# Crossing the half sums of G: one batch of the pair on ScalarE, the other on VectorE

## The chip, the cores and the metric

The kernel runs on one core of one Trainium2 chip. The metric is the device time of one execution in microseconds. Three runs of the kernel before took 2286.35, 2272.86 and 2268.79 us; their median is 2272.86.

## The reference

The input x holds 32 batches of 64 channels by 1024 positions, with one style vector of 128 numbers per batch. Four layers follow one another, each x = x + ffn(cond(x)). All four conditioning stages have the same form, four modulated 1-D convolutions of 64 channels with 3 taps:

```python
def _layer(x, style, w, b, mw, mb, typ):
    s = style @ mw.T + mb
    weight = SCALE * w * s[:, None, :, None]
    demod = lax.rsqrt(jnp.sum(weight * weight, axis=(2, 3)) + EPS)
    weight = weight * demod[:, :, None, None]
    ...
for i, typ in enumerate(('same', 'upsample', 'same', 'downsample')):
    out = _layer(out, style, weights[i], biases[i], mod_w[i], mod_b[i], typ)
```

The feed-forward stages differ: layer 0 multiplies by a 1024x1024 matrix after rounding both sides to fp8, layer 1 adds a two-of-16 expert low-rank term to a dense product, layer 2 a sparsemax mixture of 8 low-rank experts, layer 3 is a low-rank gated unit (1024 to 256 to 2 x 2752 to 256 to 1024).

## The kernel before, in words

The batches are handled in 16 pairs; a tile of 128 rows holds 64 channels of both batches, or two position parities of one batch. Each layer runs `conv_phase`, then (layers 0, 1 and 3) a phase of its own for the feed-forward part; in layers 1 and 2 the dense product is done inside `conv_phase`.

In `conv_phase` the last three convolutions of a batch are folded into one filter G, which depends on the batch. Per pair TensorE does: `conv0` (first convolution, two halves), `weights_a` and `weights_g` (products that build G; `weights_g` writes one batch's G to PSUM bank 5 and the other's to bank 6, as two half sums that lie in the other 64 rows, shifted by 64 columns), `main_half` (the filter G over the signal, 12 matmuls of 512 columns per batch), `transpose_h`, and from layer 1 on `ffn`. Every fp32 operand is split in a high and a low part (`..._hi` by ScalarE, `..._lo` by VectorE or GpSimd), and three products are summed.

The half sums of G are brought together in three steps. `cross_g` on ScalarE copies 64 rows of both banks to the other 64 rows of the SBUF tile `g_f`, twice (lines 1056 and 1057, 64x896 each). `sum_g` on VectorE (line 1239) waits for both copies and adds the banks to `g_f`, 128x1024. `split_g` then makes G's high part on ScalarE (line 1061) and its low part on VectorE (line 1243, `gl_ready`), for which `main_half` of that pair waits.

Every engine's order is written out by hand, in `iteration` of each engine's block, and waits are semaphores. In iteration p TensorE runs `main_half(p, 0)`, `weights_g(p + 1)`, `main_half(p, 1)`, half of `conv0(p + 1)`, `transpose_h(p)`, the other half, `weights_a(p + 2)` and `ffn(p)`. ScalarE: `read_a(p + 1)`, `split_x(p + 1)`, `split_z(p + 2)`, in layer 0 `quantise`, `read_h(p, 0)`, `cross_g(p + 1)`, `read_h(p, 1)`, in layer 0 `split_g(p + 1)`, `read_u(p + 1, 0)`, `split_h(p)`, `read_u(p + 1, 1)`, in the other layers `split_g(p + 1)`, `tail`. VectorE keeps the same order with its own halves of these steps, `sum_g(p + 1)` standing behind `quantise` in layer 0 and behind `split_z` elsewhere; in layer 0 `split_g(p + 1)` follows at once, and `split_h(p)` is the `hmax` reduction (line 1254) for which the next `main_half` waits (`hl_ready`).

The first pair of a layer is different. `cross_g(0)` and `sum_g(0)` stand ahead of it, and TensorE's `edges_p` (line 807) waits for `g_summed`, because it reuses banks 5 and 6. `first_pair` on VectorE then works off the edge windows (`edges_p`, `edges_v`, `edges_y`), chunks of the layer's dense weights (line 1267) or, in layer 0, the maxima of the fp8 weights, and has `sum_g(1)` between them. GpSimd makes the low part of the first chunks (line 1551) and patches edges into `hs`.

Of the kernel before, what the change touches and what calls it, by code (L numbers as in the profile page):

```python
# [29 lines left out]
ACT = mybir.ActivationFunctionType  # L30
# [5 lines left out]
P = 128  # L36
B = 32
C = 64
# [3 lines left out]
HALF = 512  # L42
# [17 lines left out]
TAPS7 = 7 * C  # L60
# [3 lines left out]
def wait_pos(eng, sem, value):  # L64

    if not isinstance(value, int) or value > 0:
        eng.wait_ge(sem, value)
# [100 lines left out]
def program(nc, d, xs):  # L168

    with ExitStack() as root:  # L170
# [12 lines left out]
        for layer in range(DEPTH):  # L183
            with ExitStack() as keep:
# [30 lines left out]
                writes_x = layer in (1, 2)  # L215
                pack = packs[layer] if layer < 3 else None
                conv_phase(nc, layer, d, xs[nbuf], xs[nbuf + 1] if writes_x else None, pack, K, kept, sem, steps, ps)
                nbuf += writes_x
                if layer == 0:
# [282 lines left out]
def conv_phase(nc, layer, d, x_src, x_dst, pack, K, kept, sem, steps, ps):  # L502
# [7 lines left out]
    g0 = NP * layer  # L510
# [4 lines left out]
    with ExitStack() as ctx:  # L515
        def sb(name, shape, dt=F32):
            return ctx.enter_context(nc.sbuf_tensor(lay + name, shape, dt))
# [14 lines left out]
        g_f = sb("g_f", [P, 2, HALF])  # L532
# [108 lines left out]
        a_done, ah_ready, al_ready = sem("a_done"), sem("ah_ready"), sem("al_ready")  # L641
        c0_done, uh_ready, ul_ready = sem("c0_done"), sem("uh_ready"), sem("ul_ready")
        g_done, gh_ready, gl_ready = sem("g_done"), sem("gh_ready"), sem("gl_ready")
        g_crossed, g_summed = sem("g_crossed"), sem("g_summed")
        m_done, hs_ready, hs_patched = sem("m_done"), sem("hs_ready"), sem("hs_patched")
        t_done, hh_ready, hl_ready = sem("t_done"), sem("hh_ready"), sem("hl_ready")
        x_loaded = sem("l0_x_loaded" if layer == 0 else "x_loaded")
# [376 lines left out]
        def _(act):  # L1024
# [27 lines left out]
            def cross_g(p):  # L1052

                act.wait_ge(g_done, 2 * (g0 + p) + 2)
                wait_pos(act, gl_ready, g0 + p)
                nc.scalar.activation(g_f[0:C, :, C:HALF], ps[C:P, 5:7, 0:TAPS7], ACT.Copy).then_inc(g_crossed, 1)
                nc.scalar.activation(g_f[C:P, :, 0:TAPS7], ps[0:C, 5:7, C:HALF], ACT.Copy).then_inc(g_crossed, 1)  # L1057

            def split_g(p):
                act.wait_ge(g_summed, g0 + p + 1)  # L1060
# [58 lines left out]
            split_x(1)  # L1119
            some_chunks(1)  # L1120
            cross_g(0)
            some_chunks(1)
            split_g(0)
# [7 lines left out]
            def first_pair():  # L1131
                some_chunks(1)
                read_a(1)
                some_chunks(1)
                split_z(2)
                read_u(1, 0)
                read_u(1, 1)
                some_chunks(2)
                act.wait_ge(ey_ready, n)
                if layer == 0:  # L1140
                    act.wait_ge(sem("p_packed_away"), 48)
                read_h(0, 0)
                read_h(0, 1)
                cross_g(1)
                if layer > 0:
                    some_chunks(1)
                else:
                    split_g(1)
                split_h(0)
                if layer > 0:  # L1150
                    some_chunks(1)
                    split_g(1)
                some_chunks(len(chunks))
                if layer > 0:
                    tail(0)

            def iteration(p, first, ahead):
                if first:
                    first_pair()
                    return  # L1160
                if ahead:
                    read_a(p + 1)
                    split_x(p + 1)
                if ahead > 1:
                    split_z(p + 2)
                if layer == 0:
                    quantise(p - 1)
                read_h(p, 0)
                if ahead:
                    cross_g(p + 1)  # L1170
                if layer == 3:
                    tail_p(p - 1)
                read_h(p, 1)
                if ahead:
                    if layer == 0:
                        split_g(p + 1)
                    read_u(p + 1, 0)
                split_h(p)
                if ahead:
                    read_u(p + 1, 1)  # L1180
                    if layer > 0:
                        split_g(p + 1)
                elif with_ffn:
                    next_weights()
                if layer > 0:
                    tail(p)
# [13 lines left out]
        def _(dve):  # L1200
# [3 lines left out]
            v = nc.vector  # L1204
# [30 lines left out]
                                       ALU.subtract).then_inc(ul_ready, 1)  # L1235

            def sum_g(p):
                dve.wait_ge(g_crossed, 2 * (g0 + p) + 2)
                v.tensor_tensor(g_f[:, :, :], ps[:, 5:7, :], g_f[:, :, :], ALU.add).then_inc(g_summed, 1)  # L1239

# [95 lines left out]
            dve.wait_ge(zeros_ready, 2 * layer + 2)  # L1336
            edges_u()
            sum_g(0)
            split_x(1)
            split_g(0)  # L1340
# [106 lines left out]
            def first_pair():  # L1447
                edges_p()
                read_a(1)
                split_z(2)  # L1450
                if layer > 0:
                    some_chunks(1)
                edges_v()
                read_u(1, 0)
                read_u(1, 1)
                edges_y()
                some_chunks(2)
                sum_g(1)
                if layer == 0:
                    split_g(1)  # L1460
                    for k in range(KB):
                        wmax(k)
                    dve.wait_ge(side[0], KB)
                    v.tensor_reduce(qm[:, 0:1], wamax[:, :], AX_X, ALU.max).then_inc(side[4], 1)
                some_chunks(1)
                split_h(0)
                if layer == 0:
                    dve.wait_ge(side[4], 2)
                    step(v.tensor_scalar(kept["w_inv"][:, :], qm[:, 1:2], 1e-12, 1.0 / FP8_MAX, ALU.max, ALU.mult))
                    v.reciprocal(wr[:, :], kept["w_inv"][:, :]).then_inc(side[3], 1)  # L1470
                else:
                    split_g(1)
                    some_chunks(len(chunks))
                    tail(0)

            def iteration(p, first, ahead):
                if first:
                    first_pair()
                    return
                if ahead:  # L1480
                    read_a(p + 1)
                    split_x(p + 1)
                if ahead > 1:
                    split_z(p + 2)
                if layer == 0:
                    quantise(p - 1)
                if ahead:
                    sum_g(p + 1)
                    if layer == 0:
                        split_g(p + 1)  # L1490
                if layer == 3:
                    tail_p(p - 1)
                if ahead:
                    read_u(p + 1, 0)
                split_h(p)
                if ahead:
                    read_u(p + 1, 1)
                    if layer > 0:
                        split_g(p + 1)
                elif with_ffn:  # L1500
                    next_weights()
                if layer > 0:
                    tail(p)
# [767 lines left out]
```

## Time and profile before

| | us |
|---|---|
| median of three runs | 2272.86 |
| profiled execution | 2273.95 |
| its span | 2272.1 |
| TensorE busy | 2043.1 (90%) |
| VectorE busy | 1192.0 (52%) |
| ScalarE busy | 880.9 (39%) |
| GpSimd busy | 428.7 (19%) |

The profile is that of one execution. The convolution phases lie roughly at 57 to 300 us (layer 0), 445 to 830 (layer 1), 1090 to 1550 (layer 2) and 1560 to 1825 (layer 3). Busy shares are averages over phases with different limits, so each place that the change touches has to be read by itself. A row's idle time is that of the engine just before the instruction, and the arrow names what ended it.

### The profile page before, as it was taken

How to read it: one execution, taken by the hardware profiler on the slowest of the kernel's cores; microseconds unless marked ns; L12 is line 12 of the kernel's file. 1: busy time of each engine (PE TensorE's matmuls, PEld its weight loads, DVE VectorE, ACT ScalarE, POOL GpSimd, SP SyncE). 2: the span in 40 equal slices, each digit the busy share in tenths (PEclk: the TensorE clock that was granted, in tenths of full speed). 3: DMA queues.
4: the chain of work that ended last, by engine and by line, in shares of the span. 5: the costliest groups of instructions: out<-in, count | busy, mean ns of one | idle time of the engine just before them, and what ended most of it. 6: DMA issues, size and time to landing. Idle time of an engine off the chain costs nothing. (4 is left out here: it accounts for less than half of the span.)

```text
span 2272.1 us, 29864 instructions
## 1 busy us (share of the span) xinstructions
PE 2043.1 (90%) x9740; PEld 1668.4 (73%) x9748; DVE 1192.0 (52%) x1999; ACT 880.9 (39%) x1352; POOL 428.7 (19%) x481
## 2 busy tenths in 40 slices
PE   2579956689999998999799999997999999979998
PEld 2458842368888886888688888876888878858886
DVE  5668769875545544232754444446555534454443
ACT  2358741144434432000433333332666644423442
POOL 4112214411001110110211111111000023352334
PEclk9889988889999998999899999997999999989999
DMA  5243314522112113222421111212111011132113
GB/s 141 84 133 100 108 51 148 189 103 69 55 55 77 61 47 120 93 92 93 144 75 55 55 55 65 73 48 80 28 37 34 22 44 48 48 111 97 43 48 152
DMA packets 98093, 180.72 MB, mean 80 GB/s; under 512 B 21120, under 2 KB 50816, under 8 KB 97280
## 3 DMA queue, kind: packets, MB, share of 16 engines
q1 hardware_dynamic: 96768, 178.16, 24.7%
q10 hardware_dynamic: 1280, 1.97, 0.4%
q8 instruction: 27, 0.44, 0.1%
q14 instruction: 18, 0.15, 0.0%
HBM read 126.02 MB, written 45.68 MB: 76 GB/s over the span
## 5 line engine op out<-in xcount | busy, mean ns | idle before, releaser
L907 PE MATMUL ps<-l_u_hi,l_g_hi 128*128 128x512 f32 x512 | 209.1, 408 | 28.8 <-DVE hmax L1254 27.6
L1065 ACT ACTIVATE l_hs<-ps,l_EY,dem3e 128x512 f32<-128x512 f32 x128 | 99.0, 777 | 296.3 <-PE ps L907 285.9
L907 PE MATMUL ps<-l_u_lo,l_g_hi 128*128 128x512 f32 x512 | 205.5, 401 | 0.0
L907 PE MATMUL ps<-l_u_hi,l_g_lo 128*128 128x512 f32 x512 | 205.0, 400 | 0.0
L119 POOL TENSOR_TENSOR l_hs<-l_EY,ones 128x4 f32<-128x4 f32 x128 | 30.7, 241 | 796.9 <-ACT l_hs L1065 796.9
L960 PE MATMUL ps<-l_w_hi,l_h_hi 128*128 128x512 f32 x512 | 167.4, 408 | 0.0
L2202 POOL TENSOR_TENSOR f_a_lo<-f_prod,f_a_hi 128x512 fp32r<-128x512 f32 (+1 forms) x88 | 113.5, 1290 | 269.4 <-ACT f_a_hi L2105 269.4
L960 PE MATMUL ps<-l_w_lo,l_h_hi 128*128 128x512 f32 x512 | 163.8, 401 | 0.0
L960 PE MATMUL ps<-l_w_hi,l_h_lo 128*128 128x512 f32 x512 | 163.0, 400 | 0.0
L2158 DVE SCALAR_TENSOR_TENSOR f_prod<-ps,b,f_gate 128x512 f32<-128x512 f32 (+1 forms) x88 | 66.0, 750 | 170.2 <-ACT f_gate L2098 170.2
L851 PE MATMUL ps<-l_x_hi,c_hi 128*128 128x512 f32 x256 | 110.5, 432 | 40.0 <-POOL l_u_lo L1533 39.7
L1233 DVE SCALAR_TENSOR_TENSOR l_u_lo<-ps,s_u,l_u_hi 128x512 fp32r<-128x512 f32 x128 | 95.6, 750 | 87.5 <-ACT l_u_hi L1049 87.3
L2031 PE MATMUL ps<-pt_hi,v_hi 128*128 128x512 f32 (+1 forms) x352 | 137.9, 392 | 1.7 <-PEq L515 1.7
L2031 PE MATMUL ps<-pt_hi,v_lo 128*128 128x512 f32 (+1 forms) x352 | 139.3, 396 | 0.0
L2031 PE MATMUL ps<-pt_lo,v_hi 128*128 128x512 f32 (+1 forms) x352 | 138.9, 395 | 0.0
L1239 DVE TENSOR_TENSOR l_g_f<-ps,l_g_f 128x1024 f32<-128x1024 f32 x64 | 78.3, 1224 | 114.9 <-ACT l_g_f L1057 114.9
L907 PEld LDWEIGHTS ps<-l_u_hi,l_g_hi 128*128 128x128 f32 x512 | 99.2, 194 | 53.7 <-issue 31.8
L2098 ACT ACTIVATE f_gate<-ps,b 128x512 f32<-128x512 f32 (+1 forms) x88 | 60.5, 688 | 180.7 <-PE ps L2031 180.7
L1049 ACT ACTIVATE l_u_hi<-ps,s_u 128x512 fp32r<-128x512 f32 x128 | 88.1, 689 | 104.1 <-PE ps L851 104.1
L1417 DVE TENSOR_TENSOR l_xr<-ps,l_xr 128x1024 f32<-128x1024 f32 x32 | 39.2, 1225 | 162.6 <-PE ps L960 108.4
L1032 ACT ACTIVATE l_x_hi<-xin,s_x 128x512 fp32r<-128x512 f32 x128 | 85.3, 720 | 97.1 <-DMA xin<-xpl 29.2
L907 PEld LDWEIGHTS ps<-l_u_hi,l_g_lo 128*128 128x128 f32 x512 | 98.8, 193 | 23.9
(332 smaller groups left out, 4960.5 us busy)
## 6 DMA issues: line engine op xcount, KB each, us to landing
xin<-x SPq DMA_DIRECT2D x96, 256.0 KB, 3.9
l_xr<-x SPq DMA_DIRECT2D x32, 512.0 KB, 4.6
x<-l_xr SPq DMA_DIRECT2D x32, 512.0 KB, 2.6
v<-in_ffn_v SPq DMA_DIRECT2D x84, 128.0 KB, 2.7
xnat<-in_x SPq DMA_DIRECT2D x16, 512.0 KB, 3.4
xin<-xpl SPq DMA_DIRECT2D x64, 128.0 KB, 2.8
l_stage<-in_ffn_w SPq DMA_DIRECT2D x16, 512.0 KB, 3.3
q_xr<-in_x SPq DMA_DIRECT2D x16, 512.0 KB, 4.0
```

The costliest lines, as they stand in the source:

```text
L851: mm = nc.tensor.matmul(ps[:, h, :], c_part[ws][:, B0 + t * P:B0 + (t + 1) * P], Xs[ms][:, h, t:t + HALF], start=(k == 0), stop=(k == 5))
L907: mm = nc.tensor.matmul(ps[:, 3 + h, :], Gs[ws][:, h, at:at + P], Us[ms][:, h, 1 + q:1 + q + HALF], start=(k == 0), stop=(k == 11))
L960: mm = nc.tensor.matmul(ps[:, 5 + o, :], hsp[ws][:, b, :], wsp[ms][:, b, o * HALF:(o + 1) * HALF], start=(k == 0), stop=(layer == 1 and k ...
L1032: nc.scalar.activation(Xs[0][:, h, 1:HALF + 1], xin[:, h, :], ACT.Copy, scale=column(s_x, p, h)).then_inc(xh_ready, 1)
L1049: nc.scalar.activation(Us[0][:, h, 1:HALF + 1], ps[:, h, :], ACT.Copy, scale=column(s_u, p, h)).then_inc(uh_ready, 1)
L1065: nc.scalar.activation(hs[:, h, :], ps[:, 3 + h, :], ACT.Identity, bias=EY[:, 1, 0, bass.ds(h * NP + p, 1)], scale=dem3e[:, bass.ds(h * NP ...
L1233: v.scalar_tensor_tensor(Us[1][:, h, 1:HALF + 1], ps[:, h, :], column(s_u, p, h), Us[0][:, h, 1:HALF + 1].bitcast(F32), ALU.mult, ALU.subt ...
L1239: v.tensor_tensor(g_f[:, :, :], ps[:, 5:7, :], g_f[:, :, :], ALU.add).then_inc(g_summed, 1)
L2031: mm = nc.tensor.matmul(ps[0:m, 2 * g + gu, :], v1sp[ws][:, s, r, gu, 0:m], pt[ms][:, r, cols], start=(k == 0), stop=(k == 5))
L2098: nc.scalar.activation(gate[0:m, g, :], ps[0:m, 2 * g, :], ACT.Silu, bias=b1[0:m, 0, bass.ds(2 * i + g, 1)]).then_inc(silu_ready, 1)
L2158: v.scalar_tensor_tensor(prod[0:m, g, :], ps[0:m, 2 * g + 1, :], b1[0:m, 1, bass.ds(2 * i + g, 1)], gate[0:m, g, :], ALU.add, ALU.mult).th ...
L2202: nc.gpsimd.tensor_tensor(asp[1][0:m, g, :], prod[0:m, g, :], asp[0][0:m, g, :].bitcast(F32), ALU.subtract).then_inc(al_ready, 1)
```

## The change

`cross_g` on ScalarE now copies only the first batch's bank (5). VectorE copies the second batch's bank (6) itself, at the head of `sum_g`, after waiting for `weights_g` to be done and for `g_f` to be free; a new semaphore `g_crossed_b` counts these copies, and the sum waits for it and for ScalarE's copies. The sum itself is the same instruction.

```diff
--- before.py
+++ after.py
@@ -641,7 +641,7 @@
         a_done, ah_ready, al_ready = sem("a_done"), sem("ah_ready"), sem("al_ready")
         c0_done, uh_ready, ul_ready = sem("c0_done"), sem("uh_ready"), sem("ul_ready")
         g_done, gh_ready, gl_ready = sem("g_done"), sem("gh_ready"), sem("gl_ready")
-        g_crossed, g_summed = sem("g_crossed"), sem("g_summed")
+        g_crossed, g_crossed_b, g_summed = sem("g_crossed"), sem("g_crossed_b"), sem("g_summed")
         m_done, hs_ready, hs_patched = sem("m_done"), sem("hs_ready"), sem("hs_patched")
         t_done, hh_ready, hl_ready = sem("t_done"), sem("hh_ready"), sem("hl_ready")
         x_loaded = sem("l0_x_loaded" if layer == 0 else "x_loaded")
@@ -1053,8 +1053,8 @@
 
                 act.wait_ge(g_done, 2 * (g0 + p) + 2)
                 wait_pos(act, gl_ready, g0 + p)
-                nc.scalar.activation(g_f[0:C, :, C:HALF], ps[C:P, 5:7, 0:TAPS7], ACT.Copy).then_inc(g_crossed, 1)
-                nc.scalar.activation(g_f[C:P, :, 0:TAPS7], ps[0:C, 5:7, C:HALF], ACT.Copy).then_inc(g_crossed, 1)
+                nc.scalar.activation(g_f[0:C, 0, C:HALF], ps[C:P, 5, 0:TAPS7], ACT.Copy).then_inc(g_crossed, 1)
+                nc.scalar.activation(g_f[C:P, 0, 0:TAPS7], ps[0:C, 5, C:HALF], ACT.Copy).then_inc(g_crossed, 1)
 
             def split_g(p):
                 act.wait_ge(g_summed, g0 + p + 1)
@@ -1235,6 +1235,11 @@
                                        ALU.subtract).then_inc(ul_ready, 1)
 
             def sum_g(p):
+                dve.wait_ge(g_done, 2 * (g0 + p) + 2)
+                wait_pos(dve, gl_ready, g0 + p)
+                v.tensor_copy(g_f[0:C, 1, C:HALF], ps[C:P, 6, 0:TAPS7]).then_inc(g_crossed_b, 1)
+                v.tensor_copy(g_f[C:P, 1, 0:TAPS7], ps[0:C, 6, C:HALF]).then_inc(g_crossed_b, 1)
+                dve.wait_ge(g_crossed_b, 2 * (g0 + p) + 2)
                 dve.wait_ge(g_crossed, 2 * (g0 + p) + 2)
                 v.tensor_tensor(g_f[:, :, :], ps[:, 5:7, :], g_f[:, :, :], ALU.add).then_inc(g_summed, 1)
```

VectorE in the last iterations of layer 0's loop, written out after it, from `quantise` (lines 1435 to 1444) over the sum (1239) and `split_g` (1243) to the `hmax` reduction (1254), before:

```order
L1435 TENSOR_SCALAR l_qm<-l_qv 128x512
L1438 TENSOR_SCALAR l_qm<-l_qm 128x512
L1441 TENSOR_TENSOR l_qv<-l_qv,l_qm 128x512
L1444 TENSOR_TENSOR wq<-l_qv,l_qm 128x512
L1239 TENSOR_TENSOR l_g_f<-ps,l_g_f 128x1024
L1243 TENSOR_TENSOR l_g_lo<-l_g_f,l_g_hi 128x1024
L1233 SCALAR_TENSOR_TENSOR l_u_lo<-ps,s_u,l_u_hi 128x512
L1254 TENSOR_REDUCE hmax<-l_hs 128x1
```

and with the change, in which line numbers behind `sum_g` are five higher:

```order
L1440 TENSOR_SCALAR l_qm<-l_qv 128x512
L1443 TENSOR_SCALAR l_qm<-l_qm 128x512
L1446 TENSOR_TENSOR l_qv<-l_qv,l_qm 128x512
L1449 TENSOR_TENSOR wq<-l_qv,l_qm 128x512
L1240 COPY l_g_f<-ps 64x448
L1241 COPY l_g_f<-ps 64x448
L1244 TENSOR_TENSOR l_g_f<-ps,l_g_f 128x1024
L1248 TENSOR_TENSOR l_g_lo<-l_g_f,l_g_hi 128x1024
L1233 SCALAR_TENSOR_TENSOR l_u_lo<-ps,s_u,l_u_hi 128x512
L1259 TENSOR_REDUCE hmax<-l_hs 128x1
```

Two copies of 64x448 stand between `quantise` and the sum; nothing else has moved.

VectorE at a layer's start (here layer 0; the others alike up to names), with the change, from the edge windows of u (1288 to 1277) to `split_g`:

```order
L1288 TENSOR_TENSOR l_ue_f<-ps,a 128x384
L1290 TENSOR_TENSOR l_ue_f<-l_ue_f,be 128x384
L1291 MEMSET l_ue_f 128x16x2
L1276 CAST l_ue_hi<-l_ue_f 128x384
L1277 TENSOR_TENSOR l_ue_lo<-l_ue_f,l_ue_hi 128x384
L1240 COPY l_g_f<-ps 64x448
L1241 COPY l_g_f<-ps 64x448
L1244 TENSOR_TENSOR l_g_f<-ps,l_g_f 128x1024
L1213 SCALAR_TENSOR_TENSOR l_x_lo<-xin,s_x,l_x_hi 128x512 x2
L1248 TENSOR_TENSOR l_g_lo<-l_g_f,l_g_hi 128x1024
```

Here the copies stand behind the last edge instruction (line 1272 before, 1277 now) and before the sum and `split_x` (1213).

## Rows read from the trace of the kernel before

**Rows 1.** Windows of layer 0's loop and layer 1's: length, engines' busy us, granted clock

```profile
160.00:290.00 130.00, 126.13 (x650) 105.95 (x649) 103.49 (x159) 103.28 (x157) 28.58 (x31) 1.00 0.37 106
560.00:830.00 270.00, 270.00 (x1360) 225.64 (x1359) 134.65 (x356) 106.35 (x173) 30.80 (x32) 1.00 0.20 62
```

**Rows 2.** The page's part 5: mean ns of one, idle before it, releaser

```profile
L1239 DVE TENSOR_TENSOR l_g_f<-ps,l_g_f 128x1024 f32<-128x1024 f32 x64 | 78.3, 1224 | 114.9 <-ACT l_g_f L1057 114.9
```

**Rows 3.** Groups of ScalarE, shapes apart: busy us, mean ns, idle before

```profile
L1056 ACT ACTIVATE l_g_f<-ps 64x896 f32<-64x896 f32 x64 | 58.6, 916 | 33.0 <-PE ps L888 32.8
...
L1093 ACT ACTIVATE l_pr<-ps 128x256 f32<-128x256 f32 x16 | 6.1, 383 | 45.9 <-PE ps L937 45.9
```

**Rows 4.** The same view of VectorE

```profile
L1384 DVE COPY l_small<-ps 128x136 f32<-128x136 f32 x16 | 4.8, 299 | 2.2 <-PE ps L942 0.7
...
L1355 DVE COPY l_small<-ps 128x80 f32<-128x80 f32 x16 | 3.8, 238 | 0.1
...
L1271 DVE CAST l_ue_hi<-l_ue_f 128x384 fp32r<-128x384 f32 x4 | 1.4, 360 | 0.1
```

**Rows 5.** Timeline of VectorE, layer 0's loop: start us, length us, [idle before]

```profile
197.15 0.88 DVE L1228 SCALAR_TENSOR_TENSOR l_a_lo<-ps,s_p,l_a_hi 128x256 fp32r<-128x256 f32 x2 [0.23 <-ACT l_a_hi L1044]
...
201.68 0.69 DVE L1444 TENSOR_TENSOR wq<-l_qv,l_qm 128x512 f32 x1
202.89 1.23 DVE L1239 TENSOR_TENSOR l_g_f<-ps,l_g_f 128x1024 f32<-128x1024 f32 x1 [0.52 <-ACT l_g_f L1057]
205.72 1.23 DVE L1243 TENSOR_TENSOR l_g_lo<-l_g_f,l_g_hi 128x1024 fp32r<-128x1024 f32 x1 [1.60 <-ACT l_g_hi L1061]
...
207.53 1.21 DVE L1254 TENSOR_REDUCE hmax<-l_hs 128x1024 f32 x1
```

**Rows 6.** Timeline of ScalarE, the same stretch

```profile
203.96 0.78 ACT L1065 ACTIVATE l_hs<-ps,l_EY,dem3e 128x512 f32<-128x512 f32 x1 [1.10 <-PE ps L907]
204.64 1.05 ACT L1061 ACTIVATE l_g_hi<-l_g_f 128x1024 fp32r<-128x1024 f32 x1
```

**Rows 7.** Timeline of TensorE: first matmul of two pairs in layer 0

```profile
159.00 0.47 PE L907 MATMUL ps<-l_u_hi,l_g_hi 128*128 128x512 f32 x1 [0.98 <-DVE hmax L1254]
...
208.88 0.47 PE L907 MATMUL ps<-l_u_hi,l_g_hi 128*128 128x512 f32 x1 [0.39 <-DVE hmax L1254]
```

**Rows 8.** Timeline of VectorE, iteration 2 of layer 0

```profile
152.89 0.69 DVE L1444 TENSOR_TENSOR wq<-l_qv,l_qm 128x512 f32 x1
153.50 1.22 DVE L1239 TENSOR_TENSOR l_g_f<-ps,l_g_f 128x1024 f32<-128x1024 f32 x1
```

**Rows 9.** Timeline of VectorE at the starts of layers 0, 1, 2 and 3

```profile
72.59 1.23 DVE L1239 TENSOR_TENSOR l_g_f<-ps,l_g_f 128x1024 f32<-128x1024 f32 x1 [2.28 <-ACT l_g_f L1057]
...
481.55 2.35 DVE L1267 TENSOR_TENSOR l_w_lo<-b_raw,l_w_hi 128x1024 fp32r<-128x1024 f32 x2
485.02 1.23 DVE L1239 TENSOR_TENSOR l_g_f<-ps,l_g_f 128x1024 f32<-128x1024 f32 x1 [1.12 <-ACT l_g_f L1057]
...
1098.70 0.56 DVE L1272 TENSOR_TENSOR l_ue_lo<-l_ue_f,l_ue_hi 128x384 fp32r<-128x384 f32 x1
1100.85 1.23 DVE L1239 TENSOR_TENSOR l_g_f<-ps,l_g_f 128x1024 f32<-128x1024 f32 x1 [1.59 <-ACT l_g_f L1057]
...
1566.10 2.58 DVE L1272 TENSOR_TENSOR l_ue_lo<-l_ue_f,l_ue_hi 128x384 fp32r<-128x384 f32 x1
1568.61 1.21 DVE L1239 TENSOR_TENSOR l_g_f<-ps,l_g_f 128x1024 f32<-128x1024 f32 x1
```

**Rows 10.** Timeline of all engines, 614.4 to 614.6 us

```profile
614.49 1.02 ACT L1075 ACTIVATE l_h_hi<-ps 128x1024 fp32r<-128x1024 f32 x1
614.51 0.75 DVE L1233 SCALAR_TENSOR_TENSOR l_u_lo<-ps,s_u,l_u_hi 128x512 fp32r<-128x512 f32 x1 [2.01 <-ACT l_u_hi L1049]
```

**Rows 11.** Timeline of all engines, 458.7 to 458.8 us

```profile
458.75 2.38 POOL L1551 TENSOR_TENSOR l_w_lo<-b_raw,l_w_hi 128x1024 fp32r<-128x1024 f32 x1 [1.35 <-ACT l_w_hi L1081]
458.76 2.92 DVE L1213 SCALAR_TENSOR_TENSOR l_x_lo<-xin,s_x,l_x_hi 128x512 fp32r<-128x512 f32 x1
```

## The prediction, made blind

> **What bounds the kernel now.** I read the windows first [rows 1]. In layer 1's loop TensorE is busy for all 270 of 270 us at full clock; the loops of layers 2 and 3 look the same. There nothing that VectorE or ScalarE does sooner can shorten the time. In layer 0's loop TensorE is busy for 126.1 of 130 us, VectorE and ScalarE for 103 each, and the timeline of TensorE says what is missing: before each pair's first matmul of `main_half` it waits 0.39 us for VectorE's `hmax` reduction [rows 7]. Four pairs lie between 159.00 and 208.88, so one takes 12.47 us. That reduction is the end of a chain: TensorE's `main_half(p, 1)`, ScalarE's `read_h` at 203.96, its `split_g` at 204.64 [rows 6], VectorE's `split_g` at 205.72, a `read_u`, the reduction from 207.53 to 208.74 [rows 5], TensorE at 208.88.
>
> The page's groups show what is changed. VectorE idles 114.9 us in front of the 64 sums of G, always for ScalarE's second crossing copy [rows 2]: most of those waits cover the two copies of 0.92 us [rows 3]. So the change can shorten almost every such wait; the question is who waits behind it. The sums matter to TensorE at two kinds of place: in layer 0's loop, through `split_g`, and at the four layer starts, where `edges_p` waits for `g_summed`, and shortly after, where the first pair's chain runs over the sum for pair 1.
>
> **Prices.** A ScalarE copy of 64x448: the 64x896 took 916 ns and a 128x256 from PSUM 383 [rows 3], so (916 - 383)/640 = 0.83 ns a column and 383 + 192 x 0.83 = 0.54 us. Both together save 2 x (0.92 - 0.54) = 0.75 us on ScalarE. A VectorE copy of 64x448 from PSUM does not occur before the change. The nearest rows are its copies from PSUM: 238 ns for 80 columns, 299 for 136 [rows 4], 1.09 ns a column; carried on to 448 that is 299 + 312 x 1.09 = 0.64 us, which I take. Below lies the SBUF rate, 0.36 us for 384 columns [rows 4], some 0.40 for 448; above, ScalarE's 0.92 for the whole 64x896, since half the columns should not cost more. Two copies and 0.03 us until the sum sees the semaphore (ScalarE's `split_g` ends at 205.69, VectorE starts at 205.72, rows 5 and 6) make 1.31 us (0.83 to 1.87). 64 pairs of copies add 82 us of work to VectorE, which is busy half of the span; what counts is where it has that time.
>
> Full-width VectorE instructions with no wait between them start some 0.08 us before the last one's end (152.89 + 0.69 = 153.58 against 153.50, rows 8). Nothing in the trace shows two half-row copies in a row; I take no overlap. With an overlap of 0.08 per copy the sum below would be about 1.6 us smaller (0.16 at each of five places, 0.08 in each of ten pairs). The Trainium skill, "VectorE: DVE Perf Modes", section "Two Vector instructions with no wait between them", speaks for no overlap: an instruction whose input or output starts in another 32-partition quadrant than the last one's is held until all earlier ones are finished, which is the case for both copies. No run here shows it yet.
>
> **Layer 0's loop.** VectorE finishes `quantise` at 201.68 + 0.69 = 202.37 and waited 0.52 us for the crossing [rows 5]. The copies now start there, and the sum at 203.68 instead of 202.89; it ends at 204.90, and ScalarE's `split_g` starts at 204.93 instead of 204.64 [rows 6], 0.29 late. ScalarE's own saving is lost: `read_h` at 203.96 waits for TensorE anyway (1.10 us idle). The delay goes on to the reduction and to TensorE. But VectorE's chain starts at `read_a` at 197.15, where it waits 0.23 us for ScalarE, which follows TensorE's `weights_a` of the iteration before [rows 5]: this path closes over two pairs, so a pair gets 0.29/2 = 0.145 us longer. VectorE's own loop would need 0.29 - 0.23 = 0.06 more, which is less. Ten pairs (iterations 4 to 13): +1.45.
>
> Iteration 2 has no such slack: the sum started at 153.50, right after `quantise`, and the 0.98 us wait of TensorE at 159.00 is already VectorE's [rows 7, 8]. The sum moves to 153.58 + 1.31 = 154.89: +1.39, passed on whole; iteration 3 then has the room of a VectorE that waits. In iteration 1 TensorE waits for GpSimd's patch of `hs` behind a DMA for longer than the delay: nothing.
>
> **Layer starts** [rows 9]. Where VectorE is idle well before g_done, the sum follows ScalarE and comes 0.75 earlier: layer 0's first (VectorE idle 2.28 us at 72.59: its copies run from 70.31 and are done first) and three more of the same pattern, layer 1's first, layer 0's and layer 3's second. What follows in layer 0 up to the loop (the reductions that let the next block of weights be loaded) is a chain behind `split_g(1)` and moves along. Four times: -3.00. Layer 2's first: VectorE is free at 1098.70 + 0.56 = 1099.26, the sum starts at 1100.57 instead of 1100.85: -0.28. Layer 1's second: VectorE is busy with `L1267` until 481.55 + 2.35 = 483.90, so the sum starts at 485.21 instead of 485.02: +0.19, and `split_h(0)`, for which TensorE's `ffn` waits, stands behind it; layer 2's second is alike, +0.19. Layer 3's first: `L1272` took 2.58 us (0.56 in layer 2, the same tile size) because of GpSimd's work beside it and ended at 1568.68; ScalarE's crossing had long been done and the sum started at once. The copies now stand in between: 1569.99 instead of 1568.61, +1.38.
>
> **Sum.** Layer 0: -1.50 + 1.39 + 1.45 = +1.34. Layer 1: -0.75 + 0.19 = -0.56. Layer 2: -0.28 + 0.19 = -0.09. Layer 3: +1.38 - 0.75 = +0.63. The FFN phases have no crossing: 0. Together +1.3 us. The profiled execution took 2273.95 us, so it would take 2275.3; the median of the three runs is 2272.86, so I forecast **2274.2 us**. One per cent, about what a measurement of this kernel can tell from no change, is 22.7 us.
>
> **Rivals.**
> Fast copies (0.40 us). Then VectorE's copies hide behind ScalarE's nearly everywhere: layer 0's loop 0 (sum ends at 204.42, before 204.64), iteration 2 +0.91, four starts -3.00, layer 2's first -0.75, two seconds -0.29 each, layer 3's first +0.90: -2.5, 2270.4 us. Against it: the two copies from PSUM in rows 4 have the slope of one column per 1.09 ns.
>
> VectorE becomes the pacer of layer 0 (slower than before). Its place is the loop, its price the copy. It decides from a copy of 0.72 us on: there the delay of `split_g`, 0.29 + 2 x (0.72 - 0.64) = 0.45, less the 0.23 of slack exceeds its half. At 0.92 us the delay is 0.85, VectorE's loop 0.62 per pair longer, +6.2; iteration 2 +1.95; layer 0's starts -0.41 - 0.75; layer 1 -0.75 + 0.75; layer 2 +0.28 + 0.75; layer 3 +1.94 - 0.75: +9.2, 2282.1 us. It would come if two engines that read PSUM at once slowed each other. Against it: ScalarE's 128x1024 and VectorE's 128x512, both out of PSUM and started 0.02 us apart, took their usual 1.02 and 0.75 [rows 10].
>
> A port race in layers 1 and 2. GpSimd's chunk started at 458.75 and took 2.38; VectorE's `split_x` started at 458.76 and took 2.92 where 0.7 is usual [rows 11]. Both follow ScalarE's crossing, so the change moves them together, but 0.01 us decides. If VectorE comes first, its chain to `gl_ready` is up to 2.2 us shorter in each of the two layers; less what TensorE cannot use, that is at most -4.4: 2269.8 us. The Trainium skill, "SBUF — State Buffer", section "Who interferes with whom", has the rule: a VectorE instruction with two SBUF inputs and a GpSimd one that reads SBUF exclude each other for the whole instruction. By that rule the trace agrees (2.92 against 0.7).
>
> The change does nothing that reaches TensorE: 2272.9 us, if iteration 2 and layer 3 find a cover that I missed.
>
> **Chances.** Forecast 0.60; nothing 0.13; fast copies 0.08; pacer 0.10; race 0.06; something else 0.03. All but the last lie within 1%: same 0.96, slower 0.03, faster 0.01. The three runs lie from 4 us below their median to 13 above, more than any of these cases, so the range is that of the cases and the runs' lower half on either side: 2268 to 2282.
>
> **What would show it.** VectorE's two new copies at 0.64 us with no overlap, ScalarE's at 0.54. In layer 0's loop a pair of 12.6 us, TensorE waiting 0.5 to 0.6 instead of 0.39, VectorE no longer waiting before the sum. In layers 1 to 3 loops VectorE's wait before the sum some 2 us shorter and TensorE unchanged. Layer 3's `edges_p` 1.4 us later behind `g_done` than before. The prediction is wrong if the loop of layer 0 does not lengthen, if the copies cost more than 0.72, or if the loops of layers 1 to 3 change length at all.

## The result, and the profile after

The changed kernel took 2281.41 us, median of 20 executions (2264.59 to 2288.90); the kernel before took 2268.76 in 20 executions beside them (2260.69 to 2290.91). The ratio is 1.0047 (95% interval 1.0028 to 1.0065): half a per cent slower, 10.7 us by the ratio, so within the 1% that I called no change. Three of all the executions told of below (2638, 7063 and 8752 us) lay far off and are left out of ranges and counts. The forecast of 2274.2 us had the class and the range right, the range by luck: 2281.41 lies 0.6 below its upper end, and that end had been set by a rival (copies of 0.92 us each) that did not come true and counted from a median of three executions that is 4.1 us above that of the 20. It had the mechanism wrong: its own sum was +1.3 us, and the loss is eight times that.

The page's part 5 after the change first. Its columns are busy us and mean ns of one, then the idle time before the group and what ended it.

```profile
L1240 DVE COPY l_g_f<-ps 64x448 f32<-64x448 f32 x64 | 40.1, 626 | 15.2 <-PE ps L888 14.3
L1241 DVE COPY l_g_f<-ps 64x448 f32<-64x448 f32 x64 | 39.6, 619 | 2.0
L1244 DVE TENSOR_TENSOR l_g_f<-ps,l_g_f 128x1024 f32<-128x1024 f32 x64 | 78.4, 1224 | 4.8 <-ACT l_g_f L1057 2.8
L1056 ACT ACTIVATE l_g_f<-ps 64x448 f32<-64x448 f32 x64 | 34.8, 543 | 33.7 <-PE ps L888 33.5
L1248 DVE TENSOR_TENSOR l_g_lo<-l_g_f,l_g_hi 128x1024 fp32r<-128x1024 f32 x64 | 98.3, 1536 | 23.8 <-ACT l_g_hi L1061 19.4
L907 PE MATMUL ps<-l_u_hi,l_g_hi 128*128 128x512 f32 x512 | 208.6, 407 | 45.8 <-DVE hmax L1259 44.7
```

What was changed does what it should. VectorE's copies take 0.62 us (0.64 taken), ScalarE's 0.54 (0.54 taken), and VectorE's idle time before the sum fell from 114.9 us [rows 2] to 4.8, with another 17.2 ahead of the two copies. But two rows that nobody touched got worse. `split_g` of VectorE took 1536 ns on average, against 1244 before; and TensorE's wait for `hmax` before `main_half` grew from 27.6 us to 44.7. These are the rows of the kernel before:

```profile
L1243 DVE TENSOR_TENSOR l_g_lo<-l_g_f,l_g_hi 128x1024 fp32r<-128x1024 f32 x64 | 79.6, 1244 | 27.4 <-ACT l_g_hi L1061 23.1
L907 PE MATMUL ps<-l_u_hi,l_g_hi 128*128 128x512 f32 x512 | 209.1, 408 | 28.8 <-DVE hmax L1254 27.6 <-DVE l_g_lo L1243 1.1
```

The second occurs in layer 0 alone. There is one pair of that loop in the timelines of VectorE, of GpSimd and of TensorE:

```profile
206.63 0.69 DVE L1449 TENSOR_TENSOR wq<-l_qv,l_qm 128x512 f32 x1
207.84 0.63 DVE L1240 COPY l_g_f<-ps 64x448 f32<-64x448 f32 x1 [0.52 <-PE ps L888]
208.49 0.62 DVE L1241 COPY l_g_f<-ps 64x448 f32<-64x448 f32 x1
209.15 1.22 DVE L1244 TENSOR_TENSOR l_g_f<-ps,l_g_f 128x1024 f32<-128x1024 f32 x1
212.55 2.86 DVE L1248 TENSOR_TENSOR l_g_lo<-l_g_f,l_g_hi 128x1024 fp32r<-128x1024 f32 x1 [2.18 <-ACT l_g_hi L1061]
...
215.99 1.20 DVE L1259 TENSOR_REDUCE hmax<-l_hs 128x1024 f32 x1
...
211.75 0.20 POOL L119 TENSOR_TENSOR l_hs<-l_EY,ones 128x4 f32<-128x4 f32 x1 [4.37 <-ACT l_hs L1065]
212.40 1.92 POOL L119 TENSOR_TENSOR xpl<-xnat,ones 128x1024 f32<-128x1024 f32 x1 [0.46 <-issue]
...
217.34 0.47 PE L907 MATMUL ps<-l_u_hi,l_g_hi 128*128 128x512 f32 x1 [2.02 <-DVE hmax L1259]
```

GpSimd's plane copy is the function `planes(p + 2)` of layer 0: SP loads a later pair's rows into `xnat` (L683), GpSimd copies them, even and odd columns apart, into `xpl` (L119), and SP spreads that into `xin`. It is the instruction ahead of which GpSimd has only its patch of `hs`. It starts at 212.40 and runs to 214.32. VectorE's `split_g` starts 0.15 us behind it and takes 2.86 us where 1.23 was usual [rows 5]. It ends 1.09 us after GpSimd's copy, as if it had begun in earnest only when GpSimd was done. The reduction, and with it TensorE, come later by as much: TensorE waits 2.02 us, against 0.39 [rows 7]. In this trace that happens in ten successive pairs, from 168.75 on. Such a pair takes 14.09 us (two of them 15.65) instead of 12.47. By the start of ScalarE's first crossing copy, the last pair of the layer is 19.55 us later than before. I call these long pairs. (`split_g` at 138.22, in iteration 1, is drawn out too, 2.32 us; in the two changed kernels with a wait, below, it is as well, 2.28 and 2.62, and no long pair follows there.)

The two pairs of 15.65 us lose the other 1.56 us on TensorE itself. Behind the wait of 2.02 us that ends at 201.68 its matmuls of 512 columns start 0.23 us apart, from 203.26 to 205.82 they start 0.43 apart, and after that 0.23 again. That is the lower of TensorE's two clock levels, 1.2 instead of 2.4 GHz. The window (length, PE busy, granted clock, DMA share, GB/s):

```profile
202.90:206.40 3.50, 3.50 (x11) 0.52 0.52 122
```

In the kernel before, whose waits in this loop are 0.39 us, the granted clock was 1.00 throughout [rows 1]. After the change the clock fell behind two of the nine waits of 2.02 us (those that end at 201.68 and 259.62) and not behind the other seven.

In the kernel before, GpSimd came second. In the pair of rows 5, `split_g` started at 205.72 and the plane copy at 206.52, because the transfer that fills `xnat` landed only then:

```profile
206.52 2.20 POOL L119 TENSOR_TENSOR xpl<-xnat,ones 128x1024 f32<-128x1024 f32 x1 [1.41 <-DMA xnat<-in_x]
```

The decisive pair is an earlier one. Here are the issue of its transfer by SP, the plane copy, and `split_g`, in the kernel before:

```profile
164.88 0.42 SPq L683 DMA_DIRECT2D xnat<-in_x  x1
...
168.31 1.22 DVE L1243 TENSOR_TENSOR l_g_lo<-l_g_f,l_g_hi 128x1024 fp32r<-128x1024 f32 x1 [1.60 <-ACT l_g_hi L1061]
...
168.44 2.88 POOL L119 TENSOR_TENSOR xpl<-xnat,ones 128x1024 f32<-128x1024 f32 x1 [0.74 <-DMA xnat<-in_x]
```

and after the change:

```profile
164.92 0.43 SPq L683 DMA_DIRECT2D xnat<-in_x  x1
...
168.75 2.82 DVE L1248 TENSOR_TENSOR l_g_lo<-l_g_f,l_g_hi 128x1024 fp32r<-128x1024 f32 x1 [1.13 <-ACT l_g_hi L1061]
...
168.57 1.92 POOL L119 TENSOR_TENSOR xpl<-xnat,ones 128x1024 f32<-128x1024 f32 x1 [0.46 <-DMA xnat<-in_x]
```

Before, VectorE was ahead by 0.13 us and it was GpSimd that stood still (2.88 instead of 1.92, which costs nobody anything). The change puts `split_g` some 0.4 us later against the transfer, and the order turns.

### The profile page after: what moved, and what is told of

The parts are those of the page before. It is cut to its first block and busy times, and to the rows that moved or that the text cites. A ratio compares the mean times of both kernels' runs of the same rounds, so it can differ in the third digit from the quotient of the medians.

```text
span 2279.6 us, 30127 instructions
## 1 busy us (share of the span) xinstructions
PE 2039.1 (89%) x9748; PEld 1665.9 (73%) x9748; DVE 1281.7 (56%) x2127; ACT 835.3 (37%) x1352; POOL 429.7 (19%) x481
## 5 line engine op out<-in xcount | busy, mean ns | idle before, releaser
L907 PE MATMUL ps<-l_u_hi,l_g_hi 128*128 128x512 f32 x512 | 208.6, 407 | 45.8 <-DVE hmax L1259 44.7
L119 POOL TENSOR_TENSOR l_hs<-l_EY,ones 128x4 f32<-128x4 f32 x128 | 34.5, 270 | 826.0 <-ACT l_hs L1065 826.0
L960 PEld LDWEIGHTS ps<-l_w_lo,l_h_hi 128*128 128x128 f32 x512 | 97.8, 191 | 23.7
```

What stands on the lines that cost most here:

```text
L907: mm = nc.tensor.matmul(ps[:, 3 + h, :], Gs[ws][:, h, at:at + P], Us[ms][:, h, 1 + q:1 + q + HALF], start=(k == 0), stop=(k == 11))
L960: mm = nc.tensor.matmul(ps[:, 5 + o, :], hsp[ws][:, b, :], wsp[ms][:, b, o * HALF:(o + 1) * HALF], start=(k == 0), stop=(layer == 1 and k ...
```

## The experiments

My theory after the traces: an order of two instructions turned in layer 0; the rival: the added work on VectorE costs everywhere. All ratios are to the kernel before, timed beside each kernel.

**The change without layer 0, and in layer 0 alone.** The new copies stand under `if layer > 0:` in the one kernel and under `if layer == 0:` in the other; the old crossing stands in the `else`:

```diff
+                if layer > 0:
+                    nc.scalar.activation(g_f[0:C, 0, C:HALF], ps[C:P, 5, 0:TAPS7], ACT.Copy).then_inc(g_crossed, 1)
+                    nc.scalar.activation(g_f[C:P, 0, 0:TAPS7], ps[0:C, 5, C:HALF], ACT.Copy).then_inc(g_crossed, 1)
+                else:
+                    nc.scalar.activation(g_f[0:C, :, C:HALF], ps[C:P, 5:7, 0:TAPS7], ACT.Copy).then_inc(g_crossed, 1)
+                    nc.scalar.activation(g_f[C:P, :, 0:TAPS7], ps[0:C, 5:7, C:HALF], ACT.Copy).then_inc(g_crossed, 1)
```

> Layer 0 crosses G as before (both batches on ScalarE), layers 1 to 3 as in the change. Port theory (the loss is layer 0's split_g on VectorE waiting behind GpSimd's plane copy): layer 0's pairs are back at 12.47 us, VectorE's split_g at 1.23 us, and the last main_half of layer 0 starts near 308 us; what is left is the gain of layers 1 to 3 that the trace of the change shows, about 5 to 6 us, so 0.997 to 0.999 of the kernel before. Load theory (VectorE's added copies cost wherever they stand): layers 1 to 3 lose too, 1.000 to 1.003.

Measured: 2263.27 us, ratio 0.9977 (0.9954 to 0.9999).

> Only layer 0 crosses G in the new way, layers 1 to 3 as before. Port theory: pairs of 14.1 us, last main_half of layer 0 some 19 us later than before; with the 6 us that the fp8 stage behind it gave back in the one profile of the change, +12 to +19 us, 1.005 to 1.008. Load theory: a third of the whole loss of 0.5%, 1.001 to 1.003.

Measured: 2284.03 us, ratio 1.0053 (1.0026 to 1.0079). So the loss is in layer 0, all of it that these intervals can tell; in layers 1 to 3 the change costs nothing measurable.

The first of these had a surprise. Of its 13 executions 12 took 2260.99 to 2268.67 us and one 2281.03, and that one was profiled. Its layer 0 is the old code, and yet:

```profile
168.94 1.92 POOL L119 TENSOR_TENSOR xpl<-xnat,ones 128x1024 f32<-128x1024 f32 x1 [0.46 <-DMA xnat<-in_x]
...
169.08 2.86 DVE L1253 TENSOR_TENSOR l_g_lo<-l_g_f,l_g_hi 128x1024 fp32r<-128x1024 f32 x1 [1.60 <-ACT l_g_hi L1065]
```

Here GpSimd was ahead by 0.14 us, and this pair and the nine after it were long. The old code can fall into the long pairs too. Its times say the same: of 118 executions of the kernel before, 105 lie between 2258.68 and 2275.33 us and 13 between 2282.78 and 2293.95, with none between. Every execution with ten long pairs in its trace took over 2281 us, every one with none under 2274.

**A wait that fixes the order.** In layer 0 the plane copy waits until `split_g` of the same pair is done, once in the changed kernel and once in the kernel before:

```diff
                 if layer == 0 and ahead > 1:
+                    if not first:
+                        pool.wait_ge(gl_ready, g0 + p + 1)
                     planes(p + 2)
```

> The change, and in layer 0 GpSimd starts the plane copy for pair p+2 only after split_g of pair p is done on VectorE (it waits for gl_ready). Port theory: split_g back at 1.23 us, pairs of 12.5 to 12.7 us, TensorE waiting 0.4 to 0.6 us for hmax instead of 2.02, last main_half of layer 0 at most 2 us later than before, total 0.996 to 1.001 of the kernel before. Load theory: pairs stay above 13.5 us, because 1.3 us of copies were added to VectorE's chain; total 1.004 or more.

Measured: 2265.07 us, ratio 0.9974 (0.9947 to 1.0001), the highest 2272.78. All the loss is gone with the change in place. In its trace the pair that turned before reads

```profile
166.93 1.22 DVE L1248 TENSOR_TENSOR l_g_lo<-l_g_f,l_g_hi 128x1024 fp32r<-128x1024 f32 x1 [1.13 <-ACT l_g_hi L1061]
...
168.48 1.91 POOL L119 TENSOR_TENSOR xpl<-xnat,ones 128x1024 f32<-128x1024 f32 x1 [2.11 <-DVE l_g_lo L1248]
```

> The kernel before with the same wait of GpSimd. Both theories: no change, 0.999 to 1.001, pairs of 12.47 us, since split_g already came first there; if the wait itself costs or gives something, it shows here.

Measured: 2266.07 us, ratio 0.9977 (0.9948 to 1.0007), the highest 2271.80. I had expected 0.999 to 1.001; the interval touches no change, but the 7 high ones among the 35 executions of the kernel before beside it have no counterpart among its 12.

**One delay in one pair.** Does the order keep itself up? The kernel before, and in layer 0 only before the sum for pair 7:

```diff
                 dve.wait_ge(g_crossed, 2 * (g0 + p) + 2)
+                if layer == 0 and isinstance(p, int) and p == 7:
+                    for _ in range(3):
+                        step(v.tensor_copy(g_f[0:C, 1, C:HALF], ps[C:P, 6, 0:TAPS7]))
```

(VectorE's loop over the pairs is cut in two around that pair, so that `p` is a number there.)

> The kernel before, with one delay in one pair: in layer 0, before the sum of G for pair 7 and only there, VectorE makes three extra copies of 64x448 that write again what ScalarE has already written (about 1.9 us). Theory 1 (two states that each keep themselves up: once GpSimd's plane copy is ahead of VectorE's split_g it stays ahead, since the longer pair lets its transfer land early): pairs of 12.47 us up to there and of 14.09 us after it, VectorE's split_g 2.8 us instead of 1.23 in seven or eight pairs, 11 to 15 us more, median 2279 to 2285 us, ratio 1.004 to 1.007, and hardly a run under 2275. Theory 2 (a delay costs itself and the pairs recover): one pair is up to 2 us longer, the later ones 12.47, ratio 1.000 to 1.001, with the same share of high runs as before (7 of 35).

Measured: 2280.45 us (2275.03 to 2283.19, 6 executions), ratio 1.0066 (1.0048 to 1.0085). The three pairs before it took 12.46 us each. Then:

```profile
200.68 1.95 DVE L1248 COPY l_g_f<-ps 64x448 f32<-64x448 f32 x3 [0.74 <-ACT l_g_f L1064]
...
205.01 2.18 DVE L1253 TENSOR_TENSOR l_g_lo<-l_g_f,l_g_hi 128x1024 fp32r<-128x1024 f32 x1 [1.12 <-ACT l_g_hi L1068]
...
218.43 2.85 DVE L1253 TENSOR_TENSOR l_g_lo<-l_g_f,l_g_hi 128x1024 fp32r<-128x1024 f32 x1 [1.60 <-ACT l_g_hi L1068]
...
204.19 1.92 POOL L126 TENSOR_TENSOR xpl<-xnat,ones 128x1024 f32<-128x1024 f32 x1 [1.29 <-DMA xnat<-in_x]
...
218.28 1.92 POOL L126 TENSOR_TENSOR xpl<-xnat,ones 128x1024 f32<-128x1024 f32 x1 [0.46 <-issue]
```

One delay of 1.95 us cost some 14: GpSimd was ahead in that pair because of it, by 0.82 us, and then in the next six pairs without any delay (one of the six took 15.64 us, with TensorE's slower level in it as above). Theory 2, that a delay costs itself, has fallen.

Why the order holds can be read from the time between SP's issue of the `xnat` load and `split_g`, beside the time until the plane copy starts, measured pair by pair:

| kernel, pairs | issue to `split_g` | issue to plane copy | ahead |
|---|---|---|---|
| before, loop from 177.94 on (9 pairs) | 2.81 to 2.85 | 3.45 to 4.13, after the transfer | VectorE |
| before, the pair at 164.88 | 3.43 | 3.56 | VectorE, by 0.13 |
| change, the same pair, two traces | 3.83, 3.82 | 3.65, 3.65 | GpSimd |
| change, the other long pairs but the last, two traces | 4.07 to 4.10, some 5.6 | 3.90 to 4.07, some 5.5 | GpSimd |

Where the plane copy waits for the transfer, it starts some 3.3 to 3.8 us after the issue in nearly all pairs. In a short pair `split_g` comes at 2.84, well ahead of that. In a long pair `split_g` comes at 4.07 or more, the data is there already, GpSimd has nothing to wait for but its patch of `hs`, and starts right behind it, which is 0.15 us ahead of `split_g`. Either order brings about the distance that keeps it. The distance grows because SP does not wait for what is late: counted from the pair's first matmul of `main_half`, `split_g` comes as before (9.34 us against 9.31), but SP's issue comes earlier (5.26 us, from 187.59 to 192.85, against 6.47, from 196.41 to 202.88). The two rows of 5.6 us are the pairs in which TensorE ran at the slower level between the issue and `split_g`.

How near the early pair is varies from execution to execution. In the kernels with the old crossing in layer 0, no wait and no copy added to every pair, the distance from issue to `split_g` there was 3.01 (the kernel of the one delay, before it), 3.43 (the kernel before) and 3.69 us (the execution above that had long pairs). In all five traces with the new copies in layer 0 it was 3.82 to 3.88.

**The wait in iterations 1 to 4 only.** GpSimd's loop in layer 0 is cut in two, `Fori(1, 5)` with the wait and `Fori(5, NP - 3)` without, in the kernel before and in the changed one.

> The kernel before; in layer 0 GpSimd's plane copy waits for VectorE's split_g of the same pair, but only in iterations 1 to 4 of 14. Theory 1 (the near tie in iteration 3, 168.31 against 168.44 us, decides for the whole loop, later the transfer lands 0.8 us behind split_g's start): the loop stays at 12.47 us a pair to its end, no run above 2275, median 2264 to 2268, ratio 0.997 to 0.999, as with the wait in all iterations. Theory 2 (the order can be lost anywhere in the loop): 1 run in 5 still above 2278.

Measured: 2265.38 us, ratio 0.9998 (0.9985 to 1.0012), the highest 2271.45; pairs of 12.47 us to the end. I had expected 0.997 to 0.999, which supposed high executions of the kernel before; it had none in its 29 beside these four kernels, so the ratio can't show what the wait saves.

> The changed kernel, with the same wait in iterations 1 to 4 of layer 0 only. Theory 1a (the change alone has too small a margin in the loop too: split_g starts at 204.98 and the transfer lands at about 205.4 in the kernel with the wait everywhere): the loop falls back into the long pairs in some iteration after 4, in most runs, median 2270 to 2280, ratio 1.001 to 1.005, with a wide spread. Theory 1b (only the early near tie is lost by the change): the loop stays at 12.6 us a pair, median 2264 to 2268, ratio 0.997 to 0.999.

Measured: 2263.72 us, ratio 0.9996 (0.9985 to 1.0008), the highest 2272.24. Theory 1b holds, but for its ratio of 0.997 to 0.999 (the same reason), and 1a has fallen: with the early pairs guarded, the one trace has no long pair in the loop, and none of the 12 executions lies among the high ones. The margin has shrunk, though. Issue to `split_g` is 3.19 us in nine pairs (2.84 before), and the plane copy started only 0.15 to 0.80 us behind, as in this one:

```profile
193.07 1.23 DVE L1248 TENSOR_TENSOR l_g_lo<-l_g_f,l_g_hi 128x1024 fp32r<-128x1024 f32 x1 [1.12 <-ACT l_g_hi L1061]
...
193.25 2.82 POOL L119 TENSOR_TENSOR xpl<-xnat,ones 128x1024 f32<-128x1024 f32 x1 [0.82 <-DMA xnat<-in_x]
```

**The delay without the change.** The kernel before with one small VectorE copy ahead of each sum of layer 0, which writes again what is there:

```diff
                 dve.wait_ge(g_crossed, 2 * (g0 + p) + 2)
+                if layer == 0:
+                    v.tensor_copy(g_f[0:C, 1, C:C + 80], ps[C:P, 6, 0:80]).then_inc(g_again, 1)
+                    dve.wait_ge(g_again, g0 + p + 1)
```

> The kernel before, whose crossing stays on ScalarE; in layer 0 VectorE writes 64 rows of 80 columns once more before each sum of G (about 0.24 us of work and 0.05 of waiting, the delay that the change gives to split_g there). Theory 1 (only the delay matters: it puts split_g behind the plane copy at the near tie of iteration 3): long pairs of 14.09 us in most executions, median 2276 to 2284 us, as with the change. Theory 2 (it is something of the change itself: its two half-row copies, or ScalarE's shorter ones): pairs of about 12.6 us, median at most 3 us above that of the kernel before.

Measured: 2272.64 us, ratio 1.0018 (0.9983 to 1.0053). Neither expectation met it. The median says little here: seven executions took 2261.60 to 2273.07 us and five 2285.06 to 2290.72. With a delay of 0.28 us the share of high executions is 5 in 12, against 13 in 118 of the kernel before (5 of 34 beside it). That speaks for the delay as a cause that needs nothing of the change, but 12 executions are few. And it is less than what the change does: 11 of 11 beside it. Why less is not shown; the traces above fit a delay that comes on top of a distance that itself varies by 0.7 us. Its profiled execution was one of the five:

```profile
169.01 1.92 POOL L119 TENSOR_TENSOR xpl<-xnat,ones 128x1024 f32<-128x1024 f32 x1 [0.53 <-DMA xnat<-in_x]
...
169.09 2.92 DVE L1246 TENSOR_TENSOR l_g_lo<-l_g_f,l_g_hi 128x1024 fp32r<-128x1024 f32 x1 [1.32 <-ACT l_g_hi L1061]
```

**The change once more.**

> The change itself once more, on the same chip as the three beside it, and a second look at its trace. Expected: long pairs in most executions, median 2278 to 2284 us, ratio 1.004 to 1.008; a transfer or a stage of the FFN that was slow in one trace by chance will not be slow in this one.

Measured: 2282.78 us (2280.77 to 2285.65, 11 executions), ratio 1.0054 (1.0032 to 1.0075), all of them among the high ones. Together with the first 20, 25 of 31 executions of the change lie at 2279.37 or above, three at 2264.59 to 2268.10, and three at 2273.90 to 2275.66, which no trace shows (the order may have turned late in the loop; that is not shown).

**The combination.** Layer 0 and layer 3's first pair cross as before, all other pairs of layers 1 to 3 as in the change, and the wait stands in all of layer 0's loop:

```diff
+                if layer > 0 and not (layer == 3 and isinstance(p, int) and p == 0):
...
+                    if not first:
+                        pool.wait_ge(gl_ready, g0 + p + 1)
```

> The combination that the runs point to: layer 0 and layer 3's first pair cross as before, all other pairs of layers 1 to 3 as in the change, and in layer 0 the plane copy always waits for split_g. By the terms of the prediction that is the kernel before with the wait (ratio 0.9977) and -0.6 us in layer 1, -0.1 in layer 2, -0.75 in layer 3: median 2262 to 2266, ratio 0.996 to 0.998; pairs of layer 0 12.47 us throughout. If it is no better than 0.9977 within the interval, the change has nothing measurable to give even where it loses nothing.

Measured: 2262.72 us, ratio 0.9987 (0.9977 to 0.9998).

> The combination once more (layer 0 and layer 3's first pair cross as before, the rest as in the change, the plane copy always waits for split_g), beside the kernel before with that wait alone. Expected: median 2260 to 2265 us, 1 to 3 us below the kernel before with the wait; if it is not below it, what it won last time came from the wait alone.

Measured: 2265.05 us, ratio 0.9966 (0.9939 to 0.9993).

> The kernel before with the wait in layer 0 alone, once more. Expected: median 2263 to 2267 us, no run above 2275; where the kernel before has no long pairs on this chip, no difference from it (ratio 0.999 to 1.001).

Measured: 2267.09 us (2259.40 to 2272.89), ratio 0.9989 (0.9966 to 1.0011). Both intervals of the combination lie below 1, the first by a hair (and above the 0.996 to 0.998 that I had expected), and beside the change it is 17.7 us faster (2265.05 against 2282.78). It is 2.0 us below the kernel before with the wait, and was 2.7 below the one with the wait in iterations 1 to 4, by medians whose executions spread over 10 us: what the change itself gives in the combination is too little to be called shown by either pair of medians. Without the high executions, though, the means point one way in all three sets of timings: 2263.6, 2262.2 and 2264.7 us with the new copies in layers 1 to 3 and the old crossing in layer 0 (the first kernel of this section and the two timings of the combination), 2267.3, 2265.4 and 2267.4 with the old crossing everywhere (the kernel before and the same with a wait). A gain of some 3 us in layers 1 to 3 is likely, then.

## Why the prediction went as it did

**The step that failed** is "Layer 0's loop": ten pairs at +0.145 us. It followed the chain through the sum and both halves of `split_g` and priced `split_g` of VectorE at its usual length wherever it would start. It took the steady pair of rows 5 for all pairs, and it did not look at GpSimd, whose plane copy starts 0.13 us behind `split_g` in the pair at 168.31. The missing term is 1.62 us in seven of ten pairs, 3.2 in two and 1.3 in one, 19.0 us together, of which 3.1 are TensorE's slower level in the two: the last crossing of the layer came 19.55 us later in the one trace of the change and 20.08 in the other. I had the mechanism as a rival, but for layers 1 and 2 only, where a race was visible because VectorE was already the loser [rows 11]; the race that VectorE was still winning has no long row to be found by. There the race paid nothing that stands out. In layer 2 of the trace of the change VectorE did come first (1112.96 against 1113.20, its two `split_x` 3.60 us together instead of 5.69), and with the change and the early wait it met no GpSimd instruction in layer 1 (1.41 instead of 5.69); from first to third crossing those starts took 53.8 and 53.9 us, others of the same layers 53.3 to 55.1 and 51.0 to 53.9.

**The mechanism of that step was right** in the short order. With the change and the early wait a pair took 12.64 us (eight pairs in 101.13 us) and TensorE waited 0.42 and 0.69 us by turns; I had said 12.6 and 0.5 to 0.6. So +0.17 a pair against the forecast +0.145. With the order kept, the changed kernel is level with the kernel before (0.9996), as the sum of +1.3 us had it.

**Layer 0 up to the loop**: right. By TensorE's first matmul of `main_half` behind the start (121.41 in the kernel before, 120.16 after), the five traces with the new copies in layer 0 are 1.4 us earlier than the nine without (119.5 against 120.9 on average; -1.50 forecast), and from there to the same matmul of iteration 3 (159.00 and 159.41) they take 1.4 us longer (39.3 against 37.9; +1.39 forecast, for iteration 2).

**No overlap of the copies**: right. They start at 207.84, 208.49 and 209.15, each behind the end of the last one. By the Trainium skill, "VectorE: DVE Perf Modes", section "Two Vector instructions with no wait between them", an instruction whose input or output starts in another quadrant of 32 partitions than the last one's is held until the earlier ones are finished. The trace agrees: 0.65 us from start to start with a length of 0.63.

**The port**: the Trainium skill, "SBUF — State Buffer", section "Who interferes with whom", calls the ports that VectorE and GpSimd share an exclusive lock, for which a VectorE instruction with two SBUF inputs contends with a GpSimd one that reads SBUF. The trace agrees in both orders: `split_g` took 2.82 to 2.86 us behind the plane copy and 1.23 alone, the plane copy 2.88 when it started 0.13 us behind `split_g` and 1.92 alone.

**Layers 1 to 3, loops**: right. From a layer's third crossing to its last the kernel before took 325.30, 345.80 and 197.81 us, the changed one 325.25, 345.80 and 197.78. Layer 1's loop after the change (length, PE busy, granted clock, DMA share, GB/s):

```profile
565.00:835.00 270.00, 270.00 (x1365) 1.00 0.21 64
```

**Layers 1 and 2, starts**: not against the forecast, as far as the traces can tell. By the starts of ScalarE's first crossing copies, seven traces with the new copies against seven without: from layer 1's first crossing to its third 52.8 against 53.5 us on average (-0.8, -0.56 forecast; single ones 51.0 to 53.9), from layer 2's first to its last 399.8 against 399.9 (-0.09 forecast; single ones 399.1 to 400.9).

**Layer 3's start**: the first step was right. `edges_p` waits 1.43 us longer (+1.38 forecast), then VectorE's `split_x` takes 1.41 instead of 2.58 us, since GpSimd is done by then. The second went further than its -0.75. In the kernel before TensorE waited 2.27 us just ahead of `ffn` and its granted clock fell right after; with a wait of 1.61 it did not. The first row of `ffn` and the window from there (length, PE busy, granted clock), before and then after:

```profile
1597.20 0.39 PE L937 MATMUL ps<-l_u_hi,l_h_hi 128*128 128x256 f32 x1 [2.27 <-DVE l_h_lo L1250]
...
1597.20:1601.40 4.20, 4.20 (x25) 0.68 0.00 0
```

```profile
1608.03 0.39 PE L937 MATMUL ps<-l_u_hi,l_h_hi 128*128 128x256 f32 x1 [1.61 <-DVE l_h_lo L1255]
...
1608.00:1611.50 3.50, 3.48 (x27) 1.00 0.00 0
```

Its 24 matmuls and the way to the next line took 4.11 us before and 2.98 after. A trace of the kernel before with the early wait repeats it (2.27 us, then 0.66), and so does the second trace of the change (1.60 us, then 1.00). In all, from its first crossing to its third, layer 3's start is 1.0 us shorter in five traces of the change (39.0 against 40.1) where I had +0.6. In the two traces of the combination it is 37.1 and 38.2. This counts only from the first crossing on; the way there from layer 2's last one varies by more (63.2 to 66.6 us over the fourteen traces).

**Where 20 us became 7.5 in the profiled executions.** The span of the profiled execution grew by 7.5 us only. Of the 12 us between, 6.1 are time that the kernel before lost in its FFN behind layer 0, in a stretch where fewer bytes came in; 4.6 are the starts of layers 1 to 3 in this pair of traces (2.6, 0.6 and 1.4). The same stretch of work before and after (length, PE busy, granted clock, DMA share, GB/s):

```profile
368.30:380.30 12.00, 5.94 (x22) 0.85 0.29 107
```

```profile
387.80:399.80 12.00, 8.73 (x33) 0.88 0.48 175
```

From the last crossing of layer 0 to the first of layer 1 that execution took 155.20 us; the thirteen other traces took 147.3 to 151.9, with the change and without. So it belongs to that one execution and is no gain of the change, as which I read it at first. What slowed the transfers there is not shown.

## What to carry to other kernels

Before adding even 0.3 us to an instruction with two SBUF inputs, list every GpSimd instruction that starts within a microsecond of it, in every pair and not only in a steady one, and ask what would happen if the order turned: a race that is being won leaves no long row. If the loser's delay makes the loop longer, check whether the longer loop lets the winner start early again; then one bad pair costs all that follow. Read the granted clock in the longer loop too: a wait that grew can cost more than its own length. Where times fall into two groups with nothing between, compare groups and their shares, and take several traces: a median between two groups describes no execution.

## What the runs showed of the hardware beyond that

- Two orders of one loop, each keeping itself up: 12.47 and 14.09 us a pair (15.65 where the clock fell) for the same instructions, chosen by some tenths of a us in one pair.
- A wait on a semaphore that only fixes an order cost nothing measurable (0.9977 and 0.9989 in the kernel before) and took the high executions away: none of the 81 executions in the seven timings with such a wait was above 2273.
- At the start of layer 3 a TensorE wait of 2.27 us was followed by a granted clock of 0.68 in the next 4.2 us, first the level of 2.4 GHz (matmuls 0.12 us apart), then that of 1.2 (0.21); with a wait of 1.61 it stayed at 1.00. In layer 0's loop after the change, waits of 2.02 us were followed by a fall to 0.52 twice in nine times, at a price of 1.56 us each. So the length of the wait alone does not say whether the clock falls. At layer 3's start, shortening the wait by 0.66 us gained 1.1 more behind it.
